# Dense rows for the heads of a routed attention, softmax sums from a column of ones, and a shorter routing chain

## What is computed

```python
h = tok(x); h = concat([cls, h])                     # (128, 17, 256)
h = h + attn(layernorm(h))                           # 16 heads of 16
x = layernorm(h)
dist = softmax(mean(x @ Wr + br, axis=1))            # (128, 16)
idx = sort(top_k(dist, 4))                           # four heads of each image
Q, K, V = (x @ W + b for the heads in idx)           # 17 x 64 each
score = softmax(Q @ K.T / 8)                         # 17 x 17 each
O = (score @ V) of the four heads, side by side      # 17 x 256
h = h + O @ Wo + bo
```

## Time and profile before

| what | value |
|---|---|
| median of 3 runs | 390.02 us (389.55 to 391.09) |
| profiled execution, whole | 390.81 us |
| its span, first to last instruction | 389.0 us |
| mean granted TensorE clock | 0.851 |
| PE busy | 314.6 us, 81% |
| DVE busy | 257.0 us, 66% |
| ACT busy | 203.2 us, 52% |
| POOL busy | 169.3 us, 44% |
| DMA | 55.97 MB in 52275 packets |

### The profile page before, as it was taken

The page is one execution under the profiler, slowest core; times in us unless marked ns, Lnnn a source line. Parts: engine busy times, 40 slices in busy tenths (PEclk is TensorE's granted clock), DMA queues, the critical chain, the costliest instruction groups (busy, mean ns, idle before and its releaser), DMA issues.

```text
span 389.0 us, 14942 instructions
## 1 busy us (share of the span) xinstructions
PE 314.6 (81%) x6334; PEld 253.9 (65%) x6334; DVE 257.0 (66%) x546; ACT 203.2 (52%) x463; POOL 169.3 (44%) x193
## 2 busy tenths in 40 slices
PE   1999999888977888785897468998889698585787
PEld 0897768535855565554795258888789687483366
DVE  2355446455578888887696776797878678462365
ACT  1023323465877777742488037777777566352320
POOL 4755000004266666642055074576657656563200
PEclk9999999999975555555698559999999999679989
DMA  7997810003500000000000068999998899824714
GB/s 206 373 424 246 248 79 0 0 0 127 199 4 5 4 3 6 3 5 3 3 2 1 0 211 266 287 289 288 258 284 272 241 286 276 249 51 97 229 54 178
DMA packets 52275, 55.97 MB, mean 144 GB/s; under 512 B 25296, under 2 KB 49008, under 8 KB 51696
## 3 DMA queue, kind: packets, MB, share of 16 engines
q1 hardware_dynamic: 51632, 52.78, 43.1%
q0 software_dynamic: 576, 2.23, 1.8%
HBM read 45.04 MB, written 9.96 MB: 141 GB/s over the span
## 4 chain that ended last, share of the span: by engine, by line
PE 37%; SPq 23%; DVE 14%; issue 10%; DMA 6%; ACT 6%; POOL 4%; POOLq 0%; ACTq 0%; DVEq 0%
SPq L457 21%; PE ps L1366 11%; PE ps L1389 5%; PE ps L1520 4%; POOL r L527 4%; DVE r L1022 4%; PE ps L1727 3%; PE ps L1449 2%; DVE rs L1032 2%; PE ps L1404 2%; PE ps L1471 2%; DVE mx L1007 2%; DMA ring<-wsplit 2%; DMA r<-in_x 2%; DMA r<-padded_rows,idx 2%
## 5 line engine op out<-in xcount | busy, mean ns | idle before, releaser
L520 POOL TENSOR_TENSOR r<-r,cst 128x1088 f32<-128x1088 f32 x16 | 33.0, 2062 | 61.6 <-DVE ring L958 58.7
L1366 PE MATMUL ps<-r 128*128 128x256 f32 x192 | 45.8, 395 | 8.6 <-DMA r<-in_x 8.6
L1366 PEld LDWEIGHTS ps<-r 128*128 128x128 f32 x192 | 37.7, 199 | 15.6 <-issue 10.5
L805 ACT ACTIVATE r<-ps 128x504 f16<-128x504 f32 (+1 forms) x50 | 31.9, 664 | 27.9 <-PE ps L1571 27.5
L1594 PE MATMUL ps<-r,ring 128*128 128x68 f16 x840 | 34.6, 201 | 12.2 <-DMA ring<-wsplit 11.3
L1471 PE MATMUL ps<-r 17*32 17x34 f32 x2048 | 30.5, 242 | 16.1 <-DVE r L1022 11.2
L1471 PEld LDWEIGHTS ps<-r 17*32 17x32 f32 x2048 | 27.3, 142 | 24.1 <-DVE r L1022 18.3
L1594 PEld LDWEIGHTS ps<-r,ring 128*128 128x128 f16 x840 | 32.1, 101 | 16.5 <-DMA ring<-wsplit 13.2
L733 ACT ACTIVATE r<-r,cst 128x136 f32<-128x136 f32 x128 | 39.9, 401 | 0.0
L609 POOL TENSOR_TENSOR r<-r,quad 128x476 f16<-128x476 f16 x38 | 37.4, 1010 | 0.6
L527 POOL TENSOR_TENSOR r<-r,rinv 128x544 f32<-128x544 f32 x16 | 18.3, 1142 | 35.3 <-DVE rinv L1036 35.3
(11 more groups left out here) (170 smaller groups left out, 696.2 us busy)
## 6 DMA issues: line engine op xcount, KB each, us to landing
ring<-wsplit SPq DMA_DIRECT2D x140, 192.0 KB, 3.3
r<-in_x SPq DMA_DIRECT2D x3, 1536.0 KB, 15.9
padded_rows<-r SPq DMA_DIRECT2D x9, 448.0 KB, 5.2
r<-in_w SPq DMA_DIRECT2D x4, 768.0 KB, 7.5
wsplit<-ring SPq DMA_DIRECT2D x1, 3072.0 KB, 11.6
r<-in_x SPq DMA_DIRECT2D x4, 384.0 KB, 8.9
h<-in_pos SPq DMA_DIRECT2D x1, 1536.0 KB, 12.1
out<-h SPq DMA_DIRECT2D x3, 512.0 KB, 2.9
```

What stands on the lines that cost most here:

```text
L520: pool.tensor_tensor(free(kx[:, u % 2, 0, :], (ROWH, UI), (NTOK, HH), (1, NTOK)), free(kr[:, 0, UI * NTOK * u:], (NTOK, UI), (0, HH), (1, ...
L1366: mm = pe.matmul(bank((n - 1) % 2, 0, D), xT[:, c, k, i * P:(i + 1) * P], tokw[:, k, :], start=k == 0, stop=k == PKT - 1)
```

## The change

1. `bd` is dense: 68 columns for each tile instead of 128, so its gaps are gone and with them their clearing on GpSimd (two memsets of 128 x 1680). The stationary operand of `weigh2` has 68 columns, and its result lies on 68 partitions.
2. V gets a 65th column of ones (high part) and zeros (low part), set once by two small memsets; each tile has a pitch of 66 columns (`VCOL`) in `v2` and in PSUM. The product of `weigh2` then has the sums of the exponentials in its 65th column. `total` and `inverse` are gone; `head_out` first inverts seven sums read from PSUM and then multiplies, on 68 partitions.
3. The rows go to `pair_rows`, dense, 17 rows for each pair. Each store is issued as two transfers, of 64 and of 4 partitions; the last step's two halves likewise, four transfers. The gather reads 4352 bytes at a row pitch of 4352 bytes (before: 8192).
4. The router's chain takes the eight largest values of `dist`, compares with the fourth, adds ties by a running count, and has running counts where masked squares stood. The order of the two counting products is swapped, and VectorE waits first for the one that it needs first. Tiles are counted in pairs (times four), by rounding with 2 to the power 25.

```diff
-PITCH = QROW * HD2
+PITCH = NTOK * HD2
+VCOL = HD2 + 2
...
-        bd = r1[:, _bd:_bd + 2 * GU * P].bitcast(F16).rearrange("p (u x g n) -> p u x g n", u=2, x=2, g=GU)
+        bd = r1[:, _bd:_bd + 2 * GU * TCOL].bitcast(F16).rearrange("p (u x g n) -> p u x g n", u=2, x=2, g=GU)
...
+        SPREAD = TCOL // 16 * 16
...
             def store_rows(v):
                 sp.wait_ge(o2_ready, 2 * (v + 1))
-                sp.dma_start(rows_of(v), o2[:, v % 2]).then_inc(o2_stored[v % 2], 16)
+                sp.dma_start(rows_of(v, 0, SPREAD), o2[0:SPREAD, v % 2]).then_inc(o2_stored[v % 2], 16)
+                sp.dma_start(rows_of(v, SPREAD, TCOL - SPREAD), o2[SPREAD:TCOL, v % 2]).then_inc(o2_stored[v % 2], 16)
...
-            for u in range(2):
-                pool.memset(free(bd[:, u, 0, 0, NTOK:], *gaps), 0.0).then_inc(bd_clear, 1)
+            for x in range(2):
+                pool.memset(free(v2[:, 0, x, 0, HD2:], (2 * GU * VCOL, 2), (VCOL, GU), (1, 1)), 1.0 - x).then_inc(ones_set, 1)
...
-                pool.tensor_tensor(free(bd[:, v % 2, x, GR * r, :], (P, GR), (QROW, IPG), (1, NTOK)),
+                pool.tensor_tensor(free(bd[:, v % 2, x, GR * r, :], (TCOL, GR), (NTOK, IPG), (1, NTOK)),
...
-            step(dve.tensor_tensor(free(sq1, *square), free(dist, *other), free(dist, *own), ALU.is_gt))
-            step(dve.tensor_tensor(free(sq2, *square), free(dist, *other), free(dist, *own), ALU.is_equal))
-            step(dve.tensor_tensor(free(sq2, *square), free(sq2, *square), tri, ALU.mult))
-            step(dve.tensor_tensor(sq1, sq1, sq2, ALU.add))
-            step(dve.tensor_reduce(rank, free(sq1, *square), AX_X, ALU.add))
-            dve.tensor_scalar(chosen, rank, float(NSLOT), None, ALU.is_lt).then_inc(mask_ready, 1)
+            step(dve.max(top[:, :], dist))
+            fourth = top[:, NSLOT - 1:NSLOT]
+            dve.tensor_scalar(over, dist, fourth, None, ALU.is_gt).then_inc(compared, 1)
+            dve.tensor_scalar(level, dist, fourth, None, ALU.is_equal).then_inc(compared, 1)
+            dve.wait_ge(compared, 1)
+            step(dve.tensor_reduce(overs, over, AX_X, ALU.add))
+            dve.wait_ge(compared, 2)
+            step(dve.tensor_tensor_scan(taken, zeros[:, :], level, overs, ALU.add, ALU.add))
+            step(dve.scalar_tensor_tensor(out=taken, in0=taken, scalar=float(NSLOT), in1=level,
+                                          op0=ALU.is_le, op1=ALU.mult))
+            dve.tensor_tensor(chosen, over, taken, ALU.add).then_inc(mask_ready, 1)
             dve.wait_ge(mask_ready, 1)
 
-            step(dve.tensor_tensor(free(sq1, *square), free(chosen, *other), tri, ALU.mult))
-            step(dve.tensor_reduce(slot, free(sq1, *square), AX_X, ALU.add))
-            dve.wait_ge(ranks_done, 2)
-            step(dve.tensor_scalar(count, bank(7, 0, NE), 1 / TP, 0.5 - 0.5 / TP, ALU.mult, ALU.add))
-            step(dve.tensor_scalar(tiles, count, ROUND, -ROUND, ALU.add, ALU.add))
-            step(dve.tensor_tensor(free(sq1, *square), free(tiles, *other), tri, ALU.mult))
-            step(dve.tensor_reduce(base, free(sq1, *square), AX_X, ALU.add))
-            step(dve.tensor_tensor(end, base, tiles, ALU.add))
+            step(dve.tensor_tensor_scan(taken, zeros[:, :], chosen, 0.0, ALU.add, ALU.add))
+            step(dve.tensor_tensor(slot, taken, chosen, ALU.subtract))
+            dve.wait_ge(ranks_done, 1)
+            step(dve.tensor_scalar(count, bank(7, 0, NE), (TP - 1) / 2, QUADS, ALU.add, ALU.add))
+            step(dve.tensor_tensor_scan(end, minus_quads[:, :], count, 0.0, ALU.add, ALU.add))
+            step(dve.scalar_tensor_tensor(out=base, in0=end, scalar=QUADS, in1=count, op0=ALU.add, op1=ALU.subtract))
...
-            def total(v):
...
-            def inverse(v):
...
             def head_out(v, r):
+                at = 2 * v + r
+                dve.wait_ge(pv2_done, at + 1)
                 if v >= 2:
+                    dve.wait_ge(o2_stored[v % 2], v // 2 * 32)
+                dve.reciprocal(rinv[0:TCOL, r, 0:GR], free(bank(weigh_bank(v, r), HD2)[0:TCOL], (VCOL, GR)))\
+                    .then_inc(rinv2_ready, 1)
+                dve.wait_ge(rinv2_ready, at + 1)
+                dve.tensor_tensor(o2[0:TCOL, v % 2, GR * r:GR * r + GR, :],
+                                  free(bank(weigh_bank(v, r))[0:TCOL], (VCOL, GR), (1, HD2)),
+                                  free(rinv[0:TCOL, r, :], (1, GR), (0, HD2)), ALU.mult).then_inc(o2_ready, 1)
...
-            pe.matmul(bank(6, 32, 32 + NE), const("before"), chosen, start=True, stop=True).then_inc(ranks_done, 1)
             pe.matmul(bank(7, 0, NE), const("one"), chosen, start=True, stop=True).then_inc(ranks_done, 1)
+            pe.matmul(bank(6, 32, 32 + NE), const("before"), chosen, start=True, stop=True).then_inc(ranks_done, 1)
...
-                        mm = pe.matmul(bank(weigh_bank(v, r), HD2 * i, HD2 * i + HD2), bd[:, v % 2, b, g, :], v2[:, v % 2, x, g, :],
-                                       start=m == 0, stop=m == 2)
+                        mm = pe.matmul(bank(weigh_bank(v, r), VCOL * i, VCOL * i + HD2 + 1)[0:TCOL], bd[:, v % 2, b, g, :],
+                                       v2[:, v % 2, x, g, 0:HD2 + 1], start=m == 0, stop=m == 2)
```

More of the change, by code:

```diff
@@ L331, in build, with rows_of @@
         HALF_PROJ = NPROJ // 2
[L332 to L334 removed]
+        SPREAD = TCOL // 16 * 16
+        def rows_of(v, first, rows, lo=0, n=GU):
+            return bass.AP(pair_rows.tensor, (v * PU + IPG * lo) * PITCH + first * HD2,
+                           [(HD2, rows), (IPG * PITCH, n), (1, HD2)])
         def stores(i):
[L338 removed]
+            return 32 * (len(range(i, NV, 2)) + (i == (NV - 1) % 2))
         LATE = 5 * 16
@@ L472, in _ @@
                 sp.wait_ge(o2_ready, 2 * (NV - 1) + lo // GR + 1)
-                sp.dma_start(rows_of(NV - 1, lo, GR), o2[:, (NV - 1) % 2, lo:lo + GR])\
-                    .then_inc(o2_stored[(NV - 1) % 2], 16)
+                for first, rows in ((0, SPREAD), (SPREAD, TCOL - SPREAD)):
+                    sp.dma_start(rows_of(NV - 1, first, rows, lo, GR), o2[first:first + rows, (NV - 1) % 2, lo:lo + GR])\
+                        .then_inc(o2_stored[(NV - 1) % 2], 16)
             STORES = ((0, 4), (4, 8), (8, 12), (12, 15), (15, 17))
@@ L1110, in _ @@
             dist, chosen, slot, count = rt[:, 48:64], rt[:, 64:80], rt[:, 80:96], rt[:, 96:112]
-            tiles, base, end, place = rt[:, 112:128], rt[:, 128:144], rt[:, 144:160], rt[:, 160:176]
-            rank, inv, at_slot = rt[:, 176:192], rt[:, 192:193], rt[:, 196:200]
+            taken, base, end, place = rt[:, 112:128], rt[:, 128:144], rt[:, 144:160], rt[:, 160:176]
+            over, inv, overs, at_slot = rt[:, 176:192], rt[:, 192:193], rt[:, 193:194], rt[:, 196:200]
+            level = rt[:, 200:216]
             in_head, span = bank(6, 32, 32 + NE), rt[:, 216:218]
@@ L1116, in _ @@
             placed = rt[:, 832 + NPAIR:832 + NPAIR + NSLOT * NE]
-            own = ((1, NE), (0, NE))
-            other = ((0, NE), (1, NE))
-            square = ((NE, NE), (1, NE))
-            tri = free(const("tri"), *square)
             dve.wait_ge(msum_done, 1)
@@ L1151, in _ @@
             step(dve.tensor_reduce(span, free(sq1, *both), AX_X, ALU.add))
-            step(dve.tensor_scalar(sq2[:, 0:NTILE], const("pair")[:, 0:NTILE], span[:, 0:1], XS, ALU.is_ge, ALU.mult))
-            dve.scalar_tensor_tensor(out=tile_head[:, :], in0=const("pair")[:, 0:NTILE], scalar=span[:, 1:2],
+            tile_pair = free(const("pair"), (TP, NTILE))
+            step(dve.tensor_scalar(sq2[:, 0:NTILE], tile_pair, span[:, 0:1], XS, ALU.is_ge, ALU.mult))
+            dve.scalar_tensor_tensor(out=tile_head[:, :], in0=tile_pair, scalar=span[:, 1:2],
                                      in1=sq2[:, 0:NTILE], op0=ALU.is_lt, op1=ALU.mult).then_inc(head_col, 1)
-            step(dve.scalar_tensor_tensor(out=place, in0=base, scalar=float(TP), in1=in_head,
-                                          op0=ALU.mult, op1=ALU.add))
+            dve.wait_ge(ranks_done, 2)
+            step(dve.tensor_tensor(place, base, in_head, ALU.add))
             step(dve.tensor_tensor(place, place, chosen, ALU.mult))
@@ L1313, in _ @@
             v_low(NV - 1, 1)
-            total(NV - 1)
             head_out(NV - 2, 1)
-            inverse(NV - 1)
             head_out(NV - 1, 0)
```

65 lines of the change are left out of this document (26 added, 39 removed).

## The result

The changed kernel takes 388.15 us (median of 16 runs, 384.94 to 391.51) against 390.90 us for the kernel before on the same chips; the ratio is 0.9912, 95% interval 0.9885 to 0.9939, so 3.4 us less by the ratio (2.4 to 4.5) and 2.75 by the medians. A second set, beside other kernels, gave 388.63 against 392.74, ratio 0.9899 (0.9862 to 0.9935), 4.0 us less. Predicted were 7.1 us. The sign was right and the size was about half.

What follows compares the result with a forecast made beforehand. Weight supply binds: DMA in steps 4 to 9; without stores DMA, SyncE and TensorE are close. Router -2.5, stores -5.0, end +0.35 make -7.15 us: 383.7 from the profiled 390.81, 382.9 against the median; 8-in-10 range 379.5 to 388.5.

Steps and rivals of the forecast that it cites:

- The router: VectorE's chain before loads and gather: shorter instructions 1.1, one product not awaited 0.44, later chain 0.92; 2.5 us saved.
- the allowance of 0.8: Router chain: running count and eight largest, absent from the trace, could together cost 0.8 us more; none of it was taken.
- The stores: Stores on SyncE's queue: fewer packets on the busiest DMA engines save 0.84 us a step, 5.0 us in six.
- that second issue: Each store's extra issue on SyncE: costed at nothing under full engines; without that cover 0.48 us a step, 2.9 in six.
- Rival (1): Small transfers fall on one engine, or steps hang on something unseen: only router and end left, 387.9 us; chance 0.13.
- TensorE's 9.6 us: TensorE's floor for a full step of 308 products, some 9.6 us, below the new pace of 11.13.
- SyncE's 9.7 us: SyncE's floor for a step with a store: 9.25 us, lengthened to 9.7 by the second issue's 0.43 + 0.05.
- The 9.73 us: Pace of a step from the first 56 loads without stores; against 11.97, a store costs 2.24 us a step.
- weigh2: Products with 65 moving and 68 stationary columns: loads hide within the 29 ns pitch, nothing taken; above 32 ns means wrong.
- rivals (3) and (4): Stationary loads in weigh2 take 57 ns: replacing the 29, 388.8 us, chance 0.09; added to it, 398 us, chance 0.05.
- The end: Chain behind the last loads: three inverses in head_out +0.65 us, last store -0.3, gather 0; net +0.35 us.
- rival (2): More comes: even spreading of packets (1.3 us more) or TensorE's clock staying full at the end (2.6 us); 380.3, chance 0.13.

Runs made afterwards that it cites:

- e2: The changed kernel without each store's transfer of four partitions, so those rows are missing in the output; 383.85 us, ratio 0.9807.
- e4: The changed kernel with a pitch of 20 rows for a pair, each store one transfer of 80 partitions; 383.98 us, ratio 0.9807.
- e1_router: The kernel before with only the new router chain, its stores, weigh2 and head_out unchanged; 387.71 us, ratio 0.9895.
- e9: The changed kernel with each step's transfer of four partitions cut from 14 tiles to one, 4 packets instead of 56; 387.46 us, ratio 0.989.
- e3: The changed kernel with the stores of steps 0 to 5 issued by ScalarE instead of SyncE; 381.22 us, ratio 0.9712.
- e6_before_act_stores: The kernel before with its stores of steps 0 to 5 issued by ScalarE, one transfer of 128 partitions each; 384.98 us, ratio 0.9876.
- e13_changed_no_loads: The changed kernel with loads for the first 21 tiles only, the others computing with what lies in the ring; 370.01 us, ratio 0.9385.
- e10: The changed kernel with 80 rows for a tile, each step's store issued as two transfers of 64 and 16 partitions; 388.68 us, ratio 0.9912.

## Why the prediction was right and wrong

**The router: right.** Predicted 2.5 us, with three parts of 1.1, 0.44 and 0.92. From the same points as in the earlier trace rows, the profile of 391.51 us (the other agrees within 0.02) has 1.42 us for the first part where 1.42 was worked out, then 0.72 from the first counting product to `count` where it was 1.15, then 0.65 where it was 1.54: 1.10, 0.43 and 0.89 saved. Eight largest cost 0.18 us, a running count 0.19 to 0.25, so the allowance of 0.8 wasn't needed. One step was missed: "tile marks are read with a stride of four, at no price that I see". They took 0.34 and 0.46 us in place of 0.29 and 0.36, 0.15 on the chain. Kept at the first load: 224.79 to 222.64, less a start of the router 0.13 later, 2.3 us.

**The stores: wrong, and here the forecast failed.** The step was that a store's 2.24 us in a step is "nearly the whole" its packets, 2.0 us, and shrinks with them. One transfer of 64, 80 and 128 partitions holds the queue 1.25, 1.7 and 2.5 us, about as its packets do; but a second one behind 64 partitions adds 1.1 to 1.2 us for 4 packets as for 224. 896 packets saved half of 2.5, and the second transfer put it back: 2.5. I had costed that second issue "at nothing", by its 0.43 + 0.05 us and under the cover of full engines, with 2.9 us in six steps "without that cover". Its price was 1.2 us of the queue each, 7 in six; leaving it out gave some 4 us of time (e2, e4). The cover went with the packets themselves, DMA from 0.93 to 0.82. With a single transfer the ratio is 0.981, some 7.5 us, near the 7.1 that I predicted, but that is in part luck: e1_router alone has 4.1 of them and the single transfer some 3.4, where 2.5 and 5.0 stood in the sum, and the intervals are 2 us wide on either side.

**Rival (1)** gave 387.9 and came true in its number, router and little else, but not by its first reason: wherever the small packets fall, they don't set the price, since 4 of them cost what 56 do (e9). Its second, "something I don't see", was the transfer itself.

**The floors.** TensorE's 9.6 us was right (9.86 without loads). SyncE's 9.7 us was wrong by the same term: 14 x 0.59 + 2.5 is 10.8 us. The other 1.4 of the measured 12.2 are loads whose issue took longer than 0.33 us, up to 1.8. These come in every kernel (1.1 us a step before, 2.3 in e3 with no store on the queue), and what stretches them is not shown; so the changed kernel is bound by SyncE's issuing, with DMA at 0.82 and no wait of SyncE for a place in the ring, but not by its stores alone. The 9.73 us that I called the pace of a step without stores was the pace of SyncE running ahead; TensorE's steps 1 and 2 took 11.1 and 11.4 us even there, so 2.24 us was not what a store costs the steps either. With stores on ScalarE the steps are still 10.8 to 11.7 us apart, and only taking the loads away brings them to 9.9.

**weigh2: "nothing" in the steps was right, its term was not nothing.** Predicted was a pitch of 29 ns or up to 3 less, with one above 32 as a sign of being wrong; measured 33 in the changed kernel, 38 with 80 columns. The float32 loads of 0.47 ns a column, which I set aside, give 32 and 38: they were the better row, and my step that float16 loads of 68 columns cost less than those of 128 "of the same kind" was wrong, as they aren't of the same kind. The rule of the Trainium skill (TensorE: Matmul & The Clock Gate, "Weight-path perf modes — Fast Weight Load (FWL) and DoubleRow") that only 128 columns load fast holds here: 97 ns against 118 for 80. The 57 ns for 68 columns that the prediction took from the same page is not borne out by the pitch of 33; rivals (3) and (4), which stood on it, did not happen.

**The end: small, as predicted.** From the start of the last weigh2 to TensorE's waking behind the stores it takes 5.59 us where it took 5.50 (352.02 to 357.52): two inverses of 0.20 each and the longer pitch, against stores that were seen 0.4 us sooner. The gather from dense rows saved about 0.5 us from there to the end of the span (31.0 for 31.5), one execution each.

**The clock in rival (2)** is real, and this change gave part of it. From 330 to 345 us TensorE was granted 0.66 before, 0.79 and 0.89 in the two profiles of the changed kernel; with its stores on ScalarE, where TensorE waited 1.8 us for loads in all, it kept the 2.4 GHz level, as it did in e6_before_act_stores. First the kernel before, then the changed kernel, then e3_act_stores:

```profile
330.00:345.00 15.00, 10.87 (x220) 9.97 (x217) 7.20 (x14) 5.78 (x13) 9.18 (x12) 0.66 0.61 175
```

```profile
330.00:345.00 15.00, 9.61 (x227) 8.80 (x223) 7.16 (x15) 6.35 (x15) 9.72 (x13) 0.89 0.54 162
```

```profile
330.00:345.00 15.00, 11.22 (x312) 10.25 (x308) 10.67 (x21) 9.45 (x24) 11.29 (x16) 1.00 0.38 101
```

What the clock is worth in the whole time no run here separates.

**Open.** Why the 56 loads ahead of the first store took 38.9 us before and between 37.4 and 42.8 in the eight profiles with the new router and stores on SyncE: the spread hides whether some of the router's lead is given back there. In the single executions nearly all of it is gone by the last products of Q and K (338.97 before, 338.91 in e1, 338.63 in the changed kernel), while the ratio of e1 keeps 4.1 us; these runs don't reconcile the two. What in a transfer costs SyncE 1.2 us is not seen either. Half of it stands in its own issue, and that half doesn't need full engines: in e13_changed_no_loads, with DMA at 0.13, the two issues of a store still take 0.58 and 0.55 us. The rest stands in whatever is next on the queue, mostly the read of the words; but such a read took up to 1.1 us in e6_before_act_stores too, where no store stood on SyncE's queue.

## What to carry to other kernels

Where a queue that only issues transfers is on the critical chain, count transfers as well as packets: ask of each one how long the queue stands still, up to the next instruction that runs at its usual time, and don't split a transfer to save packets unless that is cheaper. If engines are full and the queue waits for them, relieving the engines only helps until the queue's own cost comes up; see both floors before summing. Then try the rare transfers on another engine's queue: here that was worth more than the whole change (0.971 against 0.991 for the changed kernel, 0.988 for the kernel before).

## What the runs showed of the hardware

- A transfer of 4 packets of 256 bytes, issued behind one of 64 partitions, holds SyncE's queue for about as long as one of 224 (2.4 us for the store against 2.3, 1.25 without it): its issue takes 0.57 to 0.65 us, and the word read behind it 0.5 to 1.3 in place of 0.30 (e9, e10, the changed kernel). Where nothing holds it, an issue of a step's 128 or 80 partitions takes 0.31 to 0.43 us, one of 64, 16 or 4 takes 0.55 to 0.67.
- A store of 128 partitions drains at 218 GB/s with DMA 0.97 busy, one of 64 partitions at 154 GB/s with DMA at 0.7, so half the packets take 1.5 us (229 KB at 154 GB/s) and not 1.05. The strips, a digit and a rate for each fortieth of the stretch: the kernel before from 345.5 to 349 us, at the start of a store alone, then e2_64_rows from 341 to 345 us, one store alone:

```profile
DMA  0000000060000000000002899999999999999999
GB/s 0 0 0 0 0 0 0 0 187 0 0 0 0 0 0 0 0 0 0 0 0 59 187 243 243 222 219 225 217 217 219 214 222 219 214 219 222 211 222 214
```

```profile
DMA  0000277766767677676310000000000000000000
GB/s 0 0 0 0 54 161 154 156 151 148 156 154 154 151 161 164 138 154 143 75 21 0 0 0 0 0 0 0 0 0 0 0 0 0 0 0 0 0 0 0
```

- A float16 weight load of 128 columns is shorter (97 ns) than one of 80 (118 to 122) or 68 (115). Loading 128 and ignoring what is beyond is the faster form (pitch 31 against 38 ns), though the whole time doesn't show it.
